# Attention mask for two of four heads: from matmuls into PSUM to an accumulating DMA into the bias tile

## The reference, cut to what matters

```python
scores = jnp.einsum('bhqd,bhkd->bhqk', q / math.sqrt(HEAD_DIM), k)
scores = scores + attention_bias              # (8, 16, 512, 512) float32, one per head
scores = jnp.where(src_mask, -jnp.inf, scores)   # (8, 1, 512, 512), the same for all heads
probs = jax.nn.softmax(scores, axis=-1)
ctx = jnp.einsum('bhqk,bhkd->bhqd', probs, v)
```

## Time and profile before

| | us |
|---|---|
| median of 3 runs | 2626.97 (2624.86 to 2627.95) |
| the profiled execution's own time | 2626.6 |
| its span | 2624.8 |
| first pass, eight iterations | about 69 to 1100 |
| one iteration | 129.1 |
| TensorE busy, share of the span | 96% |
| VectorE busy, share of the span | 77% |
| GpSimd busy, share of the span | 43% |

### The profile page before, as it was taken

The page is one execution under the profiler, slowest core; times in us unless marked ns, Lnnn a source line. Parts: engine busy times, 40 slices in busy tenths (PEclk is TensorE's granted clock), DMA queues, the critical chain, the costliest instruction groups (busy, mean ns, idle before and its releaser), DMA issues.

```text
span 2624.8 us, 47276 instructions
## 1 busy us (share of the span) xinstructions
PE 2509.0 (96%) x14583; PEld 1242.2 (47%) x14583; DVE 2019.1 (77%) x3863; ACT 1147.3 (44%) x2189; POOL 1136.5 (43%) x951
## 2 busy tenths in 40 slices
PE   6999999999999999779999999999999999999996
PEld 4455555555555555434444444444444444444443
DVE  7877777777777777778878688679687786886787
ACT  3666666666676767533322223223223222232231
POOL 1464646464646464434344143343342441532430
PEclk8999999999999999989999999999999999999998
DMA  6444445454544545352322232132223222322240
GB/s 209 142 155 155 159 147 163 146 166 147 163 146 158 154 151 161 126 180 92 112 90 85 82 121 89 59 124 89 92 90 101 97 77 82 126 92 78 97 152 33
DMA packets 155507, 320.56 MB, mean 122 GB/s; under 512 B 17474, under 2 KB 23234, under 8 KB 155218
## 3 DMA queue, kind: packets, MB, share of 16 engines
q1 hardware_dynamic: 145426, 299.13, 34.9%
q10 hardware_dynamic: 9792, 17.83, 1.9%
HBM read 298.85 MB, written 17.86 MB: 121 GB/s over the span
## 4 chain that ended last, share of the span: by engine, by line
PE 42%; issue 7%; POOL 4%; DVE 4%; ACT 1%; DVEq 0%; POOLq 0%; ACTq 0%; DMA 0%
PE ffn_bank L1382 13%; PE ffn_bank L1384 13%; PE ffn_bank L1383 13%; PE ffn_bank L1368 2%; POOL x L1319 1%; POOL stage L1305 1%; POOL f L1295 1%; PE ffn_bank L1448 1%; PE ffn_bank L1389 1%; ACT g L1523 0%; DVE g2T_hi L1697 0%; DVE g2T_lo L1698 0%; DVE stage L1607 0%; DVE f L1725 0%; DVE stage L1641 0%
## 5 line engine op out<-in xcount | busy, mean ns | idle before, releaser
L1000 DVE CUSTOM_DVE_ANT_0 tiles<-bank,stage 128x512 f32<-128x512 f32 x512 | 323.9, 686 | 79.5 <-PE bank L628 74.7
L792 ACT ACTIVATE tiles<-tiles,nmax 128x512 f32<-128x512 f32 x512 | 363.5, 713 | 44.6 <-DVE nmax L1000 44.5
L508 POOL TENSOR_TENSOR stage<-stage,mask_add 128x1024 f32<-128x1024 f32 x128 | 272.1, 2137 | 202.3 <-DMA stage<-in_bias 183.0
L651 PE MATMUL bank<-ident,tiles 128*128 128x128 f32 x2048 | 300.2, 280 | 15.7 <-ACT pT L778 4.3
L1697 DVE CAST g2T_hi<-g 128x512 f16<-128x512 f32 x256 | 193.9, 757 | 154.5 <-ACT g L1523 149.0
L651 PEld LDWEIGHTS bank<-ident,tiles 128*128 128x128 f32 x2048 | 222.7, 140 | 175.5 <-issue 83.2
L1698 DVE TENSOR_TENSOR g2T_lo<-g,g2T_hi 128x512 f16<-128x512 f32 x256 | 272.1, 1063 | 8.8
L1523 ACT ACTIVATE g<-ffn_bank,bi 128x512 f32<-128x512 f32 x128 | 87.9, 687 | 361.0 <-PE ffn_bank L1384 316.5
L1382 PE MATMUL ffn_bank<-w_hi,g2T_hi 128*128 128x512 f16 x512 | 197.5, 386 | 35.1 <-DVE g2T_lo L1698 35.1
L1312 POOL TENSOR_TENSOR stage<-grid,f 128x512 f32<-128x512 f32 x64 | 104.8, 1657 | 268.1 <-DVE stage L1633 144.3
L778 ACT ACTIVATE pT<-bank 128x512 f32<-128x512 f32 x256 | 150.9, 589 | 150.4 <-PE bank L651 150.4
(11 more groups left out here) (291 smaller groups left out, 5142.4 us busy)
## 6 DMA issues: line engine op xcount, KB each, us to landing
stage<-in_bias SPq DMA_DIRECT2D x256, 512.0 KB, 4.2
stage<-in_W_l SPq DMA_DIRECT2D x128, 512.0 KB, 3.3
grid<-in_grids SPq DMA_DIRECT2D x160, 256.0 KB, 3.5
xin<-in_x SPq DMA_DIRECT2D x36, 256.0 KB, 4.0
out<-stage ACTq DMA_DIRECT2D x36, 256.0 KB, 2.0
x_rows<-tiles ACTq DMA_DIRECT2D x32, 256.0 KB, 3.0
stage<-in_W SPq DMA_DIRECT2D x16, 512.0 KB, 4.8
x2n<-x_rows SPq DMA_DIRECT2D x8, 1024.0 KB, 7.0
```

The lines of the kernel that those rows point to most:

```text
L508: pool.tensor_tensor(bias[:, n % NB, :, :], bias[:, n % NB, :, :], mask_add[:, u % T, :].unsqueeze(1).to_broadcast([P, 2, S]), ALU.add).th ...
L651: mm = pe.transpose(bank[:, t * P:(t + 1) * P], tiles[:, 4 * (u % NR) + i, t * P:(t + 1) * P], ident[:, :])
L792: act.activation(tile, tile, ACT.Exp, scale=-1.0, bias=nmax[:, u % 2, i:i + 1], accum_out=rsum[:, j, h:h + 1]).then_inc(prob_ready, 1)
L1000: dve.tensor_tensor_reduce(tiles[:, 4 * (u % NR) + i, :], bank[:, :], bias[:, half % NB, i % 2, :], -1.0, 3.0e38, ALU.add, ALU.min, nmax[: ...
```

## The change

PE no longer adds a mask: the two identity matmuls per slot and the wait for `mask_ready` go, and all four score products start a bank. For the odd tile of each slot POOL waits until it has landed and then issues a DMA that adds `mask_add` to it, with the bfloat16 source read twice (once for each head) and the float32 destination accumulated. This comes ahead of POOL's own work on the even tile of the same slot. Three semaphores in turn count the landings, and DVE waits for them ahead of head 2 where it waited for the load.

```diff
+        SUMS = [len(range(n, NQ, 3)) for n in range(3)]
...
+        mask_summed = [sem(f"mask{i}_summed") for i in range(3)]
...
                 pool.wait_ge(mask_ready, it * 1 + 1)
                 for u in range(NQ):
+                    n = 2 * u + 1
+                    pool.wait_ge(bias_in[n % NB], (it * USES[n % NB] + n // NB + 1) * 16)
+                    pool.sem_inc(pool_carrier, 1)
+                    pool.dma_start(bias[:, n % NB, :, :], mask_add[:, u % T, :].unsqueeze(1).to_broadcast([P, 2, S]),
+                                   accum_op=ALU.add).then_inc(mask_summed[u % 3], 16)
                     n = 2 * u
                     pool.wait_ge(bias_in[n % NB], (it * USES[n % NB] + n // NB + 1) * 16)
                     pool.tensor_tensor(bias[:, n % NB, :, :], bias[:, n % NB, :, :],
...
                 def scores(u):
                     g, j = u // T, u % T
-                    if u == 0:
-                        pe.wait_ge(mask_ready, it * 1 + 1)
...
                     for i in range(4):
-                        bank = claim(pe, it, ("S", u, i))
-                        if i >= 2:
-                            pe.matmul(bank[:, :], ident_bf[:, :], mask_add[:, j, :], start=True, stop=False)
-                    for i in range(4):
                         rows = slice(HD * i, HD * i + HD)
+                        claim(pe, it, ("S", u, i))
                         pe.matmul(psum[i][:, :], q32[rows, g, j * P:(j + 1) * P], k32[rows, g, :],
-                                  start=i < 2, stop=True).then_inc(full[i], 1)
+                                  start=True, stop=True).then_inc(full[i], 1)
...
                             if i == 2:
-                                dve.wait_ge(bias_in[half % NB], (it * USES[half % NB] + half // NB + 1) * 16)
+                                dve.wait_ge(mask_summed[u % 3], (it * SUMS[u % 3] + u // 3 + 1) * 16)
```

## The result

The changed kernel takes 2724.64 us (2722.57 to 2732.89, four runs) against 2627.46 for the kernel before beside it: a ratio of 1.0379, 95% interval 1.0359 to 1.0399. It is 97 us slower; 2592 was forecast, and the range ended at 2657. The profiled execution took 2732.89 us of its own, with a span of 2731.0, so its rows show some 8 us more than the median.

The account below looks back on a forecast made before the run. TensorE was taken as the bound, then GpSimd's stream: of the 66.6 us that removing the matmuls allowed, 35 would remain, landing and traffic costing nothing. 2627 - 35 = 2592 us, range 2560 to 2657.

Parts of the forecast that it names:

- the fourth rival: Lock between GpSimd and VectorE: each GpSimd issue held up 1.66 us, iteration 7.2 us longer, 2685 us; chance 0.06.
- Part 2: GpSimd's stream, slots 9 to 15, with 16 issues an iteration: bounds the gain to 4.4 us an iteration, 35 in all.
- c: Time one DMA issue holds GpSimd's stream: taken as 1.34 us, between 0.54 and 2.13.
- the prediction's own formula: GpSimd's chain to slot 15 lets an iteration end 13.8 - 7c us earlier, c being one issue's time; TensorE's work allows 8.3.
- the same sum: GpSimd's work from slot 9 on plus its issues: in slots 10 to 14 fewer issues, delay absorbed by loading three slots ahead.
- Part 1: Mask matmuls leave TensorE: 0.52 us in each of 128 slots, 66.6 us in all; 54 from below.
- Parts 3 and 4: The mask DMA's landing, covered up to 4.4 us, and its traffic, 8 MB more writes an iteration: both taken at no cost.
- L: Time from issue to landing of the mask's DMA: taken as 4.2 us, at most 7.0, which would cost 21 us.
- I take none: Cost of late bias tiles from added DMA traffic: taken as none, though each us late would cost 8 us.
- The signs named in advance: Gap ahead of GpSimd's adds, shorter VectorE score waits, TensorE idle some 4 us more around slots 15 and 16, iterations near 124.7.

Follow-up runs that it names:

- y4: The changed kernel with GpSimd's add cut to one column of each head, the accumulating DMA whole: 2621.08 us, ratio 0.9975.
- w1: The changed kernel with GpSimd's add replaced by fifteen tiny adds of one column for each head, the accumulating DMA whole: 2662.78 us, ratio 1.0135.
- x1: The changed kernel without the accumulating DMA, so heads 2 and 3 stay unmasked: 2600.69 us, ratio 0.9901.
- y3_small: The changed kernel with the accumulating DMA cut to 16 of each head's 512 columns: 2757.94 us, ratio 1.0509.

## Why the prediction was wrong

By the ratios the way from before to after is: matmuls gone, -26; issues and transfers (y4), +19; GpSimd's time (w1), +42; the hold (changed), +64. The steps depend on their order, since a stall in one slot gives the engines behind it time. The +19 is net: y4 has the DMA, but lacks the add and its hold, which alone shortens slot 3 by 0.85 us against x1. No run cut the add without the DMA, so the issues and transfers cost more than 19, and part of the 64 is hold that x1 had too. It was forecast as -67, no cost, +32 and none.

**The hold.** This is the step that failed. It stood as the fourth rival with a chance of 0.06, and "Against it: on DVE the casts are few beside that stretch of POOL's stream" looked at GpSimd as the one held up. It was the other way, as the row had shown, and the place was above all not slots 9 to 15 but the start of the iteration, where GpSimd runs three slots on end and VectorE has the expert's weights ahead of slot 0's first head; slot 13 came second. That the price could be more than one add, 9.4 us for 1.66, no row of before showed. The rule of the Trainium skill, "SBUF — State Buffer", section "SBUF: two separate sides", gives the ports that the two share, where both need them, to whichever instruction starts first, for the whole of it, and blocks the other fully. The trace agrees that one blocks the other; what happens where GpSimd's issue and add overlap the rule leaves open, and there 9.38 us outlast three adds.

**Part 2, GpSimd's chain.** c is 2.87 - 2.12, the distance of two slots after and before: 0.75 us, within the bounds and below the 1.34 taken. By the prediction's own formula that frees the whole 66.6 us, so the formula is wrong, not c. "In slots 10 to 14 the same sum runs but with fewer c and the delay is absorbed" failed: the first chain of statistics at slot 9 was near its limit, and ScalarE, with TensorE behind it, stopped there (4.86 us in w1_filler_15). The odd tile, taken to land 3.7 us after slot 6 was scored, landed 4.3 to 4.6 after it before the change and 4.5 to 7.7 in the changed kernel (7.4 in the iteration of w1_filler_15 shown).

**Part 1.** The term was 66.6 us and measured 26. The distance is 0.43 us, nearer the lower bound, and slots 1, 9 and 13 were already limited by ScalarE or VectorE; slot 3 and the stretch behind slot 15 gained nothing either, and for those two no row shows why. The window of the iteration averages these away; slots 11 to 14 were looked at, the others not.

**Parts 3 and 4.** L is 6.2 us, between the 4.2 taken and 7.0. VectorE waited 9 us for it in the whole pass, so it hardly mattered by itself. Traffic: the share rose from 0.48 to 0.71, as forecast, and bias tiles land in 4.5 to 5.0 us for 4.2. "I take none" for a late bias tile failed in one place: slot 9's odd tile, ahead of the statistics, took 6.0 us for 4.3, and with y3_small's transfers, where it took 4.4, slot 9 was 2.9 us shorter (6.66 for 9.52). What that is worth in all no run shows.

**The signs named in advance.** The gap on POOL ahead of an add is 0.78 us from issue to add; iterations did not go to 124.7. DVE's wait for score products hardly shrank (74.7 to 73.4 us). TensorE's idle time grew by 9.7 us in the iteration looked at, not 4, and not around slots 15 and 16.

Open: why the hold outlasts the add when an issue overlaps it. GpSimd's records are rough, and no run here separates a port that is kept from a turn that is lost. Nor was it separated how much of GpSimd's 42 us is the clock, and how much of slot 9 is traffic.

## What to carry to other kernels

Before giving GpSimd's queue a DMA, list VectorE's instructions that read and write SBUF alone and stand ahead of something TensorE needs; if one lasts until a GpSimd add ends already, an issue that overlaps that add can multiply it. Price a removed TensorE instruction slot by slot, with each slot's next-busiest engine, not from the window of an iteration. Where a change helps some slots and hurts others, make it in those slots alone.

## What the runs showed that was not expected

- A VectorE instruction of 0.28 us took 9.38 us beside three issues and three adds of GpSimd; beside adds alone its neighbours of 0.23 and 0.35 us took 2.0, beside issues and one tiny add each it took 0.30, beside issues and fifteen tiny adds 0.41 (medians).
- An accumulating DMA of 512 KB holds GpSimd's stream for 0.75 us beside an add and lands in 6.2 us (6.7 to 7.0 with GpSimd's adds small, 8.9 with twice as many, 3.4 for 16 of 512 columns).
- After 2.43 us of idleness TensorE ran at 0.50 of its clock from about 655 to 661.7 us, with 0.63 us for matmuls that take 0.38 at the full clock.
- A reciprocal written to 128x512 from a broadcast source took 3.35 us, a copy of that size 0.43.
